# Order of three steps in a cross-attention kernel: x1 + bias before the lower halves on GpSimd, the mask earlier on ScalarE, the turned context later on VectorE

## The reference

```python
# part 1
Mn = Wn @ inorm(x) + bn;  Mm = Wm @ inorm(ctx) + bm
A  = softmax(Mn^T Mm)                       # 512 x 512
x1 = Wo @ ((Wl @ ctx + bl) A^T) + bo + x
# part 2
q = layer_norm(x1) @ q_w + q_b;  k = ctx @ k_w + k_b;  v = ctx @ v_w + v_b
scores = q k^T / sqrt(32), masked along the keys
hidden = softmax(scores) v @ cproj_w + cproj_b + x1
out = hidden + gelu(layer_norm(hidden) @ fc_w + fc_b) @ proj_w + proj_b
```

## Time and profile before

| | us |
|---|---|
| median of 3 runs | 3034.43 |
| lowest and highest | 3033.48 and 3048.21 |
| the profiled execution | 3045.41 |
| its span in the trace | 3043.6 |
| PE busy | 2862.2 (94%) |
| DVE, ACT, POOL busy | 1880.3, 1495.3, 1121.4 |

### The profile page before, as it was taken

How to read it: one execution, slowest core, us unless ns; L and a number is a source line. 1 busy time by engine, 2 the same in 40 slices (tenths; PEclk the granted TensorE clock), 3 DMA queues, 4 the chain that set the end, 5 groups by cost and what they waited for, 6 DMA issues and landing times. The chain is left out here.

```text
span 3043.6 us, 54525 instructions
## 1 busy us (share of the span) xinstructions
PE 2862.2 (94%) x17527; PEld 2370.5 (78%) x17527; DVE 1880.3 (62%) x3642; ACT 1495.3 (49%) x4274; POOL 1121.4 (37%) x998
## 2 busy tenths in 40 slices
PE   5899999999999999999976999999999999999999
PEld 4777777777777777777765888888888888888887
DVE  5788888888888888888865433333333333333332
ACT  5788877888788887888753211111111111111111
POOL 4566666666666666666642000000000000000000
PEclk7899999999999999999997999999999999999999
DMA  6588888888888888888764211101111111111110
GB/s 188 161 231 224 230 223 240 229 236 229 234 235 234 232 225 236 235 232 232 213 188 141 70 28 28 38 31 41 41 41 41 28 28 37 32 41 41 41 28 14
DMA packets 440891, 416.66 MB, mean 137 GB/s; under 512 B 155201, under 2 KB 319553, under 8 KB 440769
## 3 DMA queue, kind: packets, MB, share of 16 engines
q1 hardware_dynamic: 440768, 415.40, 49.6%
HBM read 231.79 MB, written 167.77 MB: 131 GB/s over the span
## 5 line engine op out<-in xcount | busy, mean ns | idle before, releaser
L1346 ACT ACTIVATE gl<-pre,fc_bias 128x512 f32<-128x512 f32 x256 | 176.6, 690 | 1118.9 <-PE pre L1431 1118.9
L1385 DVE CAST hT_hi<-gl 128x512 fp32r<-128x512 f32 x256 | 109.1, 426 | 838.6 <-ACT gl L1346 838.6
L685 ACT ACTIVATE rows<-bank,negmax 128x128 f32<-128x128 f32 x1024 | 365.1, 395 | 126.7 <-DVE negmax L865 126.7
L607 POOL TENSOR_TENSOR at_lo<-a_blocks,at_hi 128x512 fp32r<-128x512 f32 x256 | 338.7, 1345 | 192.5 <-ACT at_hi L730 192.5
L593 POOL TENSOR_TENSOR rows<-rows,rsum 128x512 f32<-128x512 f32 x256 | 266.6, 1042 | 272.9 <-DVE rsum L861 272.8
L177 POOL TENSOR_TENSOR rstd<-ve,neghalf 128x4 f32<-128x4 f32 x16 | 16.3, 1019 | 869.0 <-DVE ve L171 869.0
L1429 PE MATMUL pre<-yT_lo,rest_hi 128*128 128x512 f32 x768 | 298.8, 389 | 0.0
L1430 PE MATMUL pre<-yT_hi,rest_lo 128*128 128x512 f32 x768 | 298.8, 389 | 0.0
L1431 PE MATMUL pre<-yT_hi,rest_hi 128*128 128x512 f32 x768 | 298.8, 389 | 0.0
L1429 PE MATMUL acc<-rest_lo,hT_hi 128*128 128x512 f32 x768 | 298.8, 389 | 0.0
L1430 PE MATMUL acc<-rest_hi,hT_lo 128*128 128x512 f32 x768 | 298.8, 389 | 0.0
(11 more groups left out here) (159 smaller groups left out, 7891.8 us busy)
## 6 DMA issues: line engine op xcount, KB each, us to landing
a_turn<-rows SPq DMA_DIRECT2D x128, 512.0 KB, 7.6
a_blocks<-a_turn SPq DMA_DIRECT2D x256, 256.0 KB, 5.1
p_turn<-rows SPq DMA_DIRECT2D x128, 512.0 KB, 5.0
p_blocks<-p_turn SPq DMA_DIRECT2D x256, 256.0 KB, 5.8
x_ctx<-in_x SPq DMA_DIRECT2D x64, 256.0 KB, 2.7
x_ctx<-in_ctx SPq DMA_DIRECT2D x64, 256.0 KB, 2.9
blocks<-in_ctx SPq DMA_DIRECT2D x256, 64.0 KB, 5.6
small<-in_x SPq DMA_DIRECT2D x64, 256.0 KB, 6.0
```

Source lines behind the costliest of these rows:

```text
L607: pool.tensor_tensor(by_rows(at_lo, j), a_chunks[:, j], by_rows(at_hi, j).bitcast(F32), ALU.subtract).then_inc(at_lo_set, 1)
L685: act.activation(probs[:, :, r, c, :], by_chunk(S1_BANK[r])[:, c, :].rearrange("p (d b) -> p d b", b=32), ACT.Exp, bias=negmax1[:, r, c:c ...
L1346: act.activation(gl[:, i % 2, :], pre[i % 2][:], ACT.Gelu_apprx_tanh, bias=mlp.fc_bias[:, i:i + 1]).then_inc(gelu_done, 1)
```

## The change

Three blocks are moved, with their waits; nothing is added and nothing removed. Instruction counts of every engine stay. On POOL `lower_normed()` of a slot that isn't filling goes behind `x1_rstd` and `x1b`. On ACT the mask goes from behind `upper_normed` to behind `outT_hi`. On DVE the turning of ctx goes from in front of `x1` to behind `hid`.

```diff
@@ gpsimd, slot
                 lower_at(0)
                 lower_at(1)
-                if not filling:
-                    lower_normed()
                 if b1.exists():
                     pool.wait_ge(x1_veps, b1.nth(1, 1))
...
                     pool.tensor_tensor(x1b[:, b1.quarter, :], x1[:], cproj_bias[:], ALU.add).then_inc(x1b_set, 1)
+                if not filling:
+                    lower_normed()
                 if a1.exists():
                     pool.wait_ge(ctxT_hi_set, a1.nth(1, 1))
@@ scalar, slot
                 if b5.exists() and not b4.exists():
                     first_weights(1)
+                if b3.exists():
+                    if b3.first():
+                        act.wait_ge(consts_set, 4)
+                    act.wait_ge(mask_loaded[b3.parity], b3.dma())
+                    if b3.has_before(1):
+                        act.wait_ge(s1_done, (b3 + -1).nth(1, 1))
+                    act.activation(mask_less_1[:], mask_u8[:, b3.parity, :], ACT.Identity,
+                                   bias=minus_one[:]).then_inc(mask_set, 1)
                 if filling:
                     upper_normed()
@@ vector, slot
                 turn_a(3)
...
-                if a1.exists():
-                    dve.wait_ge(blocks_in, a1.nth(64, 64))
-                    if b1.exists():
-                        dve.wait_ge(ctxT_lo_set, b1.nth(1, 1))
-                    dve.transpose(ctx_chunks.rearrange("p c (r b) -> p c r b", b=32),
-                                  blocks[:].rearrange("p (r c b) -> p c r b", c=DC, b=32)).then_inc(ctxT_turned, 1)
                 if b1.exists():
                     dve.wait_ge(out0_done, b1.nth(1, 1))
...
                     dve.tensor_tensor(hid[:], bank[C_BANK][:], x1b[:, b5.quarter, :], ALU.add).then_inc(hid_set, 1)
+                if a1.exists():
+                    dve.wait_ge(blocks_in, a1.nth(64, 64))
+                    if b1.exists():
+                        dve.wait_ge(ctxT_lo_set, b1.nth(1, 1))
+                    dve.transpose(ctx_chunks.rearrange("p c (r b) -> p c r b", b=32),
+                                  blocks[:].rearrange("p (r c b) -> p c r b", c=DC, b=32)).then_inc(ctxT_turned, 1)
```

More of the change, by code:

```diff
@@ L777, in slot @@
                     upper_normed()
[L778 to L785, removed]
                 if a1.exists():
```

## The result

The changed kernel is slower: 3081.2 us (3076.39 to 3084.94) against 3039.3 us (3033.48 to 3048.21) for the kernel before, four executions each; ratio 1.013, interval 1.011 to 1.015. I had forecast 3017.5 us, 2985 to 3046. The two profiled spans, 3074.5 and 3043.6 us, are 30.9 us apart.

What follows compares the result with a forecast made beforehand. The first ring, about 23.7 us, shrinks to 22.5, so the second bounds at 23.62: 56 x (23.87 - 23.62) = 14 us, plus 3 in the first slots, 17 us off 3034.43 gives 3017.5 us, range 2985 to 3046.

Steps and rivals of the forecast that it cites:

- The ordinary slot: Steady attention slot after the change: 23.55 us, with spread 23.62, instead of 23.87.
- `normed_lo` behind `x1b`: On POOL: `x1b` ends near 1023.2 instead of 1025.09, before the maxima are done; gains DVE's 0.89 us per slot.
- The length of `x1n`: On DVE: `x1n` starts earlier but is held by POOL's running `normed_lo`, up to 1.26 us; PE's 0.84 us wait still goes.
- Late slots: Slots where late `a_blocks` made `normalise_inputs` collide with POOL's `at_lo` (2.01 instead of 0.98 us); the collision should go.
- The first slots: At the start PE waited up to 4.1 us for the mask, twice; perhaps 3 us come back.
- Rival 1: DMA transfers asked for earlier also finish earlier, PE bounds at 22.46 us per slot: 2952 us, half way 2985; chance 0.13.
- Rival 2: On ACT the mask's late landing delays scaling and `u_hi`: slot 24.0 to 24.2 us, 3050 us; chance 0.12.
- Rival 3: The second ring already bounds the kernel before, the mask's 0.2 us eating the rest: 3031 to 3037 us; chance 0.25.
- the second ring: SP's load, `p_blocks`, `a_turn`, `a_blocks`, DVE's turning and normalising, next load: 23.35 us, 23.55 with the mask's 0.2.
- The first ring: DVE, ACT and POOL waiting in a circle through `x1n`, PE beside it: about 23.7 us, shrinking to 22.5.
- What would show it: Signs: PE's `x1n` and mask waits gone, DVE waiting for `a_blocks` 60 to 90 us per run, load to load 23.5 to 23.7.

Runs made afterwards that it cites:

- the two cut writes: On the kernel with `ctxT_hi` moved over the jump, 384 KB per item left out of `a_turn` (2986.1 us) or of `p_turn` (3025.9 us).
- the kernel without the stall: The changed kernel with ACT's `ctxT_hi` made first in the next slot, so the jump stands ahead of its wait: 3030.5 us, ratio 0.996.
- the new SP order: SP's next load moved behind the write of `a_turn`: 3034.4 us on the kernel before, 2984.4 us on the one with `ctxT_hi` over the jump.

## Why the prediction was wrong, point by point

- **The step that failed**: "*`ctxT_hi` on ACT comes 2 to 3 us later, into idle time before the second softmax. Zero.*" The idle time before `exp1` was read from the profile as waiting for maxima. In one slot of four it was also the cover of the code fetch behind the jump. In both kernels `ctxT_hi`'s wait stands in front of the jump and the jump follows 0.10 us behind the turning of ctx; the edit made the turning, and with it the jump, 3 to 4 us later against the maxima. Its price was 4.25 us x 12 = 51 us, against a forecast gain of 17. Moved alone it costs 48 us; with the block taken back nothing of it is left, and with `ctxT_hi` moved across the jump some 5 us. The question of what is queued behind a waiting instruction I answered with the next compute instruction; the jump stood between.
- **The ordinary slot** was nearly right: 23.73 us in the kernel with `ctxT_hi` over the jump, where 23.55 to 23.62 stood. (The 23.59 of the changed kernel holds one slot of 23.0 behind each stall, so its nearness to the forecast is partly luck.) Load to the start of `turn_a` is 19.84 us (12.1 + 7.6 = 19.7 forecast), from there to the load 3.85 (3.65 + 0.2 for the mask). The mask was there 0.4 us behind `a_blocks`, as taken, and 5.3 us behind its own issue. That this ring bounds is shown by the two cut writes.
- **`normed_lo` behind `x1b`**: right. In the slot of 1016 us `hid` ends at 17.33, `x1b` at 18.70, `x1n` starts at 19.04 behind two maxima and waits for nobody.
- **The length of `x1n`**: right. Each of POOL's two `normed_lo` has its own record: the first runs from 1018.66 to 1019.95, `x1n` from 1019.04 to 1020.22, 0.27 us behind its end, and the second `normed_lo` takes 1.47 us instead of 1.29. It was 0.28 us behind `ctxT_lo` before. The Trainium skill's rule that I had set beside it (SBUF — State Buffer, Who interferes with whom) agrees: held to the end of the other's running instruction. The gain comes from the earlier start, as said.
- **Late slots**: right in kind, and I undersold it. That the mask ahead of scaling keeps `at_lo` off `normalise_inputs` is worth 1.2 us per slot where it would otherwise always collide (3101 against 3030 us).
- **The first slots** gave 8.2 us, not 3. The stretch behind the 61st `x1n` got 3.8 us longer, and 3.1 in the kernel with `ctxT_hi` over the jump; I had nothing for it and haven't followed it. Without the stall the sum would have been 56 x (23.87 - 23.73) = 8 us and 7 in the first slots, less 3 at the end: 12 us, the difference of the two spans (3043.6 and 3032.0), where I had 17. Of the slots alone it is 8 us where I had 14.
- **Rival 1** (the ring gives way, 2952 to 2985) was out: it gives way to another order of SP's queue, not by itself. **Rival 2** named slower for the wrong reason; its mask wait was as small as I took it. **Rival 3** stood with times (3031 to 3037) against a kernel before of 3034.43 us, so as 3 us gained to 3 lost; the kernel without the stall gained 10 us by the medians of its chip (3030.5 against 3040.1) and 12 by the spans, about midway between that and the 17 of the forecast. That the kernel before wasn't bound by the second ring alone, nor by the first, shows in that either one opened by itself brings 0.4%, and both bring 2.0%. The first ring, opened, is 22.87 us or less (22.46 forecast).
- **What would show it**: `a_blocks` waits 99.5 us in 49 slots (60 to 90 forecast), PE for `u_lo` 56.0 in 50, the mask's DMA 123.0 in 48, all of the kind listed. So the list of signs for "right" was met by a kernel that got slower; no item of it looked at the loop's end.

## What to carry to other kernels

Before moving a wait towards the end of a loop body, look at what stands behind it on that engine including the jump back, and read one slot at each place of the loop rather than a mean slot: a cost that comes every fourth time is invisible in the mean and plain in a sorted list. Where waits of two rings are nearly equal, opening one shows next to nothing; try the second on top before judging the first.

## What was unexpected in the hardware

- **A jump back costs a code fetch that queues with the data.** Over the 12 jumps the 8 KB for ACT began 1.1 to 2.7 us behind the jump (mean 2.0) in the kernel before and 3.4 to 6.2 us behind it (mean 5.0) in the changed one, where loads, `p_blocks` and `a_turn` had just been issued; ACT ran on 1.5 to 2.1 us later in both. One pair of runs changed nothing but the order of the data transfers: with the new SP order on the kernel before, the packet begins 3.0 to 4.2 us behind the jump (mean 3.6) instead of 2.0. So what is in the queues does delay it; that this is the whole of the 5.0 us isn't shown. The same pair shows that the length of the fetch alone isn't the cost: ACT ran on 5.2 us behind the jump there instead of 3.7, and the slots behind a jump were no longer than the others (23.60 and 23.69 us). The Trainium skill, Advanced Engine Details and Errata, Control Flow Timing, gives about 108 ns for a compare-and-branch: by it the jump would be free, and here it is 3.1 to 4.3 us to the next instruction in the kernel before and 5.3 to 7.7 us in the changed one. The same page, Sequencer Loop, says that engine instructions wait in a queue while the sequencer reads on; that is how the jump at 1019.85 could precede `normed_hi`. What holds the sequencer back here is a wait that isn't met yet: in both kernels the jump comes 0.10 us behind the end of DVE's turning of ctx.
- **A longer loop body can eat up what its saved jumps bring**: eight slots instead of four brought 40 code packets of 16 KB in 600 us where there were none, and 0.55 us more in each slot without a jump. The kernel was still 13 us faster than the changed one, where 30 us of stalls were saved.
- **A wait of 2.7 us per slot can be worth keeping**: with the mask's moved behind `at_hi`, `normalise_inputs` takes 2.4 us instead of 1.1 (2 x 1218 and 2 x 539 ns), held by POOL's `at_lo`.
